# Second norm's row gather two ticks earlier, its statistics in the middle of a chunk, in a two-layer gated cross-attention kernel

## The reference

```python
x = x + jnp.tanh(g_xattn[0]) * _L0_xattn_ref(_layernorm(x, axis=-1), ctx_1024, ctx_1024, ...)
x = x + jnp.tanh(g_ffn[0]) * _L0_ffn_ref(_layernorm(x, axis=-1), ...)
x = x + jnp.tanh(g_xattn[1]) * _L1_xattn_ref(_layernorm(x, axis=-1), ctx_1024, ...)
x = x + jnp.tanh(g_ffn[1]) * _L1_ffn_ref(_layernorm(x, axis=-1), ...)
```

## Time and profile before

| | before |
|---|---|
| median of 3 runs | 1305.31 us (1303.09 to 1306.69) |
| the profiled execution | 1305.32 us |
| its span | 1303.6 us |
| PE busy | 1113.0 us (85%) |
| DVE busy | 1010.9 us (78%) |
| POOL busy | 637.0 us (49%) |
| ACT busy | 586.5 us (45%) |
| mean granted clock of PE | 0.959 of full speed |

### The profile page before, as it was taken

How to read it: one execution, slowest core, us unless ns; L and a number is a source line. 1 busy time by engine, 2 the same in 40 slices (tenths; PEclk the granted TensorE clock), 3 DMA queues, 4 the chain that set the end, 5 groups by cost and what they waited for, 6 DMA issues and landing times.

```text
span 1303.6 us, 23736 instructions
## 1 busy us (share of the span) xinstructions
PE 1113.0 (85%) x7464; PEld 960.2 (74%) x7464; DVE 1010.9 (78%) x2393; ACT 586.5 (45%) x1506; POOL 637.0 (49%) x377
## 2 busy tenths in 40 slices
PE   5145544899969998799889999999999999999998
PEld 3133333789858988688788888889888888888887
DVE  2999999989999899898537444445688888888887
ACT  2212222465636555355454645454344444444443
POOL 4889997898788987899340110101011111111200
PEclk9999985799989999799899999999999999999999
DMA  6101112889748886589666255552000000000000
GB/s 226 49 25 41 40 41 73 264 269 284 224 151 263 278 253 208 187 240 294 189 198 206 78 176 160 174 162 79 22 25 25 25 25 25 26 25 25 26 9 17
DMA packets 125035, 166.41 MB, mean 128 GB/s; under 512 B 10032, under 2 KB 67568, under 8 KB 124912
## 3 DMA queue, kind: packets, MB, share of 16 engines
q1 hardware_dynamic: 119792, 152.31, 38.1%
q0 software_dynamic: 5120, 12.59, 2.9%
HBM read 137.60 MB, written 27.26 MB: 126 GB/s over the span
## 4 chain that ended last, share of the span: by engine, by line
PE 56%; DVE 25%; issue 8%; POOL 7%; ACT 2%; DMA 1%; SPq 0%; DVEq 0%; POOLq 0%; ACTq 0%
PE ZB L1276 8%; DVE q_sb L898 6%; PE YB L1290 6%; PE YD L1328 5%; DVE s L873 4%; PE ZD L1244 4%; PE ZD L1246 4%; PE ZD L1245 4%; POOL prod L586 3%; PE YB L1328 3%; PE ZB L1244 2%; DVE own_prod L862 2%; PE ZB L1246 2%; PE ZB L1245 2%; POOL xs L596 2%
## 5 line engine op out<-in xcount | busy, mean ns | idle before, releaser
L562 POOL TENSOR_TENSOR rstd<-ve,neghalf 128x4 f32<-128x4 f32 x64 | 65.6, 1025 | 516.6 <-DVE ve L827 515.2
L683 ACT ACTIVATE hid<-ZB,w2b 128x128 f32<-128x128 f32 x768 | 215.8, 378 | 159.0 <-PE YB L1290 78.5
L574 POOL TENSOR_TENSOR prod<-q_sb,kv_sb 128x2048 f32<-128x2048 f32 x48 | 216.3, 4507 | 51.9 <-DVE q_sb L898 31.6
L586 POOL TENSOR_TENSOR prod<-s,kv_sb 128x2048 f32<-128x2048 f32 x48 | 215.2, 4505 | 10.6 <-DVE q_sb L898 10.5
L1276 PE MATMUL ZB<-bt,w1b 128*128 128x128 f32 x1536 | 213.2, 284 | 4.9 <-ACT hid L683 4.7
L1276 PEld LDWEIGHTS ZB<-bt,w1b 128*128 128x128 f32 x1536 | 197.0, 200 | 8.5 <-issue 8.0
L1290 PE MATMUL YB<-w2b,hid 128*128 128x128 f32 x1024 | 141.4, 282 | 0.0
L1290 PEld LDWEIGHTS YB<-w2b,hid 128*128 128x128 f32 x1024 | 129.1, 194 | 14.2 <-ACT hid L683 8.0
L705 ACT ACTIVATE own_prod<-ZD 128x512 f32<-128x512 f32 x102 | 61.1, 599 | 154.6 <-PE ZD L1246 152.3
L1095 DVE TENSOR_TENSOR prod<-own_prod,ZD 128x512 f32<-128x512 f32 x102 | 69.5, 682 | 75.0 <-ACT own_prod L705 51.7
L1110 DVE SCALAR_TENSOR_TENSOR own_prod<-YD,gate,own_prod 128x128 f32<-128x128 f32 x320 | 89.7, 342 | 46.5 <-PE YD L1328 44.6
(11 more groups left out here) (249 smaller groups left out, 2321.0 us busy)
## 6 DMA issues: line engine op xcount, KB each, us to landing
w2b<-in_w SPq DMA_DIRECT2D x96, 516.0 KB
w1b<-in_w SPq DMA_DIRECT2D x96, 512.0 KB
xb<-xs SPq DMA_DIRECT2D x96, 128.0 KB
ctx_t<-in_ctx SPq DMA_DIRECT2D x32, 256.0 KB
x2d<-x2s SPq DMA_DIRECT2D x48, 128.0 KB
x<-in_x SPq DMA_DIRECT2D x16, 256.0 KB
xs<-zrow SPq DMA_DIRECT2D x4, 1024.0 KB, 10.5
xrow<-in_x SPq DMA_DIRECT2D x16, 256.0 KB, 3.6
```

Source lines behind the costliest of these rows:

```text
L574: pool.tensor_tensor(out=prod[:, t % 2, :].rearrange("p (h e d) -> p h e d", h=HEADS, e=HEADS), in0=q.unsqueeze(2).broadcast_to([P, HEADS, ...
L586: pool.tensor_tensor(out=prod[:, (t + 1) % 2, :].rearrange("p (h d e) -> p h d e", h=HEADS, e=HEADS), in0=s0[:, t, :, :].unsqueeze(2).broa ...
L683: act.activation(hid[n % 2][:, j, k * RT:(k + 1) * RT], ZB[j // 2][:, at:at + RT], ACT.Relu, bias=w2b[t % 3][:, k, e, FJ * D + j:FJ * D + ...
```

## The change

The gather is issued two ticks earlier (kc = -6 and -5), POOL's small norm one tick earlier (kc = -2), and DVE's statistics move from kc = -2, even half, to kc = -4, odd half. `_ready` in the table of start ticks is raised by two.

```diff
@@ -72,7 +72,7 @@
-    _ready = max(h for h, (b, _) in PLACE.items() if b == BLOCK_OF[_c]) // 2 + 5
+    _ready = max(h for h, (b, _) in PLACE.items() if b == BLOCK_OF[_c]) // 2 + 7
     C0.append(max(_ready, C0[-1] + 8 if C0 else 8 * (NC + 1)))
@@ -95,7 +95,7 @@
 def c_parts(tick):
-    return [(c, tick - C0[c]) for c in range(NC) if -4 <= tick - C0[c] < 8]
+    return [(c, tick - C0[c]) for c in range(NC) if -6 <= tick - C0[c] < 8]
@@ -615,7 +615,7 @@
                     for c, kc in c_parts(tick):
-                        if kc == -1:
+                        if kc == -2:
                             norm(2, c)
@@ -631,9 +631,9 @@
                     for c, kc in c_parts(tick):
-                        if kc == -4:
+                        if kc == -6:
                             gather(c, (0, 1))
-                        if kc == -3:
+                        if kc == -5:
                             gather(c, (2, 3))
@@ -1187,10 +1187,6 @@
                     for c, kc in c_parts(tick):
-                        if kc == -2:
-                            for j in range(TILES):
-                                dve.wait_ge(ld_x2[j].sem, ld_x2[j].at(c))
-                            norm_stats(2, lambda j: x2[c % 2][:, j, :], c)
                         if kc == 2:
                             biased(BVV, vv_sb, "vv", c)
@@ -1202,6 +1198,10 @@
                             logits_max(d)
                     for c, kc in c_parts(tick):
+                        if kc == -4:
+                            for j in range(TILES):
+                                dve.wait_ge(ld_x2[j].sem, ld_x2[j].at(c))
+                            norm_stats(2, lambda j: x2[c % 2][:, j, :], c)
                         if kc == 1:
                             score_max(c)
```

## The result

The changed kernel takes **1326.34 us** (median of 4 runs, 1318.66 to 1329.51) where the kernel before took 1306.0 beside it (1303.09 to 1307.68): ratio 1.0144, 95% interval 1.0123 to 1.0164, that is 18.8 us (16.1 to 21.4) more. The forecast was 1314.8 with a range up to 1319.0. The sign was right, the forecast rise (9.5 us) about half of what came, and the time lies above the range. The profiled execution took 1324.97 us.

What follows compares the result with a forecast made beforehand. PE was taken to set the pace in the last stage (97% busy), any hold on it paid in full. 1305.3 - 4.0 (front) + 13.5 (last stage), chunks 1 to 5 at 0, gave 1314.8 us, range 1309.0 to 1319.0.

Steps and rivals of the forecast that it cites:

- The last stage, +13.5 us: Ten chunks: statistics delay unit 7's product and PE; nine chunks at 1.40 us plus 0.9 for the first; 10.8 to 14.5.
- none of the 1.46 us is absorbed, nine of ten alike: Last stage: nine of ten chunks have no DVE gap between L1019 and unit 7's product, so all pay.
- Rival 1: Last stage: DVE's idle 18% swallows the 1.46 us, only the front counts, faster at 1301.3 us; chance 0.08.
- rival 2: Last stage: earlier statistics remove PE's 0.56 us wait for xn in ten chunks, giving 1309.2 us; chance 0.06.
- Rival 3: Last stage: a 1.3 us wait in each chunk lowers PE's clock, 2.2 us more in ten chunks, 1336.8; chance 0.03.
- Rival 4: Front: gathers land as late relative to DVE as before, scatters standing between, no gain, 1318.8 us; chance 0.03.
- The front, chunk 0, -4.0 us: First attention to cross attention: PE reaches L1391 2.8 us earlier, plus 1.2 us for the clock; -1.5 to -5.0.
- the last of eight such DMAs starts 7 x 1.27 us after 598.67: Front, POOL's queue: last gather starts at 607.6, rows usable at 611.8, DVE waits about 1.5 us in place of 4.89.
- my 3.7: Front, chunk 0: PE's new wait for DVE's later work, 0.73 + 3.0 = 3.7 us.
- let DVE hide by half: Front: a clock drop behind PE's new wait is half hidden by PE waiting for DVE anyway; 1.2 us counted.
- Chunks 1 to 5, cost 0: While experts run: statistics ahead of x2s still leave it made in time; otherwise 1.46 us in each of four chunks.

Runs made afterwards that it cites:

- last_only: Kernel before with the whole change for chunks 6 to 15 only, chunks 0 to 5 as before: 1319.01 us, 1.0098.
- pos4: Kernel before with chunks 6 to 15 alone altered: statistics right behind the value bias, in DVE's idle gap, gathers at kc = -9 and -8: 1305.76 us, 0.9996.
- c0_only: Kernel before with the whole change for chunk 0 alone: 1304.85 us, 0.9986.
- c0_spread: Kernel before with chunk 0 alone changed, its gathers still earlier (kc = -8, -7), a POOL product between and behind the pairs: 1304.47 us, 0.9982.
- c1_kept: Kernel before with the change for chunks 0 and 2 to 5, chunk 1 and chunks 6 to 15 as before: 1304.06 us, 0.9991.
- all_but_c1: Changed kernel with chunk 1 alone as in the kernel before: 1319.15 us, 1.0097.
- c0_and_c1: Kernel before with the whole change for chunks 0 and 1 only: 1311.12 us, 1.0039.
- eight_in_a_row: Kernel before with four added gathers into an unread tile behind the real four from chunk 8 on, making runs of eight: 1346.69 us, 1.0303.
- c1_to_5: Kernel before with the whole change for chunks 1 to 5, chunk 0 as before: 1309.31 us, 1.0008.
- gather_only: Kernel before with only POOL's gathers moved in all chunks, norm and statistics where they were: 1306.71 us, 1.0006.
- c1_gather_only: Kernel before with the whole change for chunk 0 and only the gathers moved for chunk 1: 1312.01 us, 1.0045.
- front_only: Kernel before with the whole change for chunks 0 to 5, chunks 6 to 15 as before: 1313.36 us, 1.0048.
- spread: Kernel before with the change for chunks 0 to 5, but their gathers further ahead (kc = -8, -7); chunks 6 to 15 as before: 1313.83 us, 1.0059.
- no_two_port: Kernel before with the change for chunks 0 to 5, where nmean and ve are made by scalar_tensor_tensor in place of tensor_scalar: 1315.56 us, 1.0058.
- combined: Kernel before with chunk 0 as in c0_spread, chunks 1 to 5 as before, chunks 6 to 15 as in pos4: 1303.22 us, 0.9982.

## Why the prediction was right in part and wrong in size

**The last stage, +13.5 us: right.** last_only measured 12.8 us and the trace 13.0. The step "none of the 1.46 us is absorbed, nine of ten alike" held: chunks of 33.74 against the 33.7 named, 1.41 us each against 1.40. The first chunk cost 0.35 in place of 0.9, since DVE's gaps took up 0.94 us and not 0.5. The matmuls took 1.13 where I had 1.16. pos4 shows the reason by its opposite: it is the place ahead of a product that PE asks for 0.12 us later, not the ten instructions.

**Rival 1 (all hidden) and rival 2 (the xn wait given back)** are excluded by the nine new waits at L1328 and by the xn wait that stays. **Rival 3 (the clock falls in the last stage)** is excluded: nine waits of 1.2 us, and 1.00 throughout. The rule of the Trainium skill, TensorE: Matmul & The Clock Gate, section A second HAM failure mode: psum-queue depth-cycling, did not apply to idles of this size and spacing. **Rival 4 (the gathers land too late)** is excluded as well: the first statistics start at 608.03 us without a wait.

**The front, chunk 0, -4.0 us: right in sign, too large.** c0_only measured -1.8 (-3.7 to -0.1). The 4.89 us wait is gone and L1391 is not held, but L1391 is not nearly 3 us earlier: counted from the landmark at 601 us it comes 1.1 us later in the changed kernel. (Only c0_spread, whose gathers stand elsewhere, has it at 627.09, where I had 627.2; that is luck.) Three prices were missing. I had worked out that "the last of eight such DMAs starts 7 x 1.27 us after 598.67", so I had the run of eight before me, and charged it to POOL alone; ACT stood 6 us beside it, and PE waited 5.48 us in place of my 3.7. The half speed behind that wait, 0.55 from 609 to 618 us or 4.1 us of work, I had let DVE hide by half; the rank matmul then found its tile ready, so nothing was hidden. And nmean, taken at 0.17 us from the steady rows, met POOL's product, whose place I had in the earlier trace rows, and took 2.69 us. What is left as a gain is that L1391 now runs at full speed, where it stood at the head of a slow stretch before. The windows do not settle how much: the profiled execution of c0_only was its slowest, 1309.21 us.

**Chunks 1 to 5, cost 0: this is the step that failed.** It holds for chunks 2 to 5 as long as chunk 1 stays (c1_kept). For chunk 1 it is wrong by 6 to 7 us: 6.1 from all_but_c1, and (1.0039 - 0.9986) x 1306 = 6.9 from c0_and_c1 against c0_only. I had asked there only where the statistics stand on DVE (ahead of x2s, whose reader comes later) and had not followed chunk 1's four gathers through POOL's queue, where they now stand around chunk 14's scatters. My own steps had even brought these scatters forward, by making pick_slots 3.4 us early (629.72 to 626.3). The terms as measured apart: -1.8 for chunk 0, +6.9 for chunk 1, 0 for chunks 2 to 5 and +12.8 make +17.9, against 18.8 (16.1 to 21.4) measured.

**What stays open.** That eight indirect transfers in a row stop the other engines is shown, in the last stage alone and in the front; by what they do it is not. The trace of the changed kernel has no load of instructions from 598 to 612 us, and that of eight_in_a_row none from 1063 to 1070, so that isn't it. That chunk 0 and chunk 1 must both move for the loss is shown (c1_to_5 and c0_only against c0_and_c1), and that it takes chunk 0's statistics and chunk 1's gathers (gather_only against c1_gather_only). That this is because chunk 14's scatters then close up to the gathers ahead of them, and because PE no longer has its wait for pick_slots to hide a standstill in, is what the traces suggest (POOL's pause between the first two gathers and the scatters is 1.1 us in front_only, 2.7 in gather_only and in c1_to_5), but no run separates the two.

## What to carry to other kernels

An instruction that moves takes its own queue with it: follow every transfer that the step issues, and look at what will stand next to it there, not only at who waits for its data. Short work on an engine that is 18% idle is free or costs its full length depending on whether the next tile it delays has a reader at the door, so look for the gap, then for the reader. And where a trace shows engines idle for "remote" on a kernel of one core, look at what the other engines were issuing in that moment.

## What the runs showed of the hardware that I had not expected

- A run of eight indirect transfers from POOL, 1.27 us apart, stops ACT, DVE and PE from about the fifth on: 4.95 us a run in the last stage with the DMA engines 0.11 busy, lower clock included, and 2.3 to 6.1 us of ACT in the front. With a pause of 2.8 us after four, 0.7 us are left. Four in a row stop ACT too, for 1.8 us in three places of the kernel before.
- A DVE instruction on four elements a partition takes as long as POOL's running product still has: 1.6 to 3.4 us for nmean and once 4.5 for ve, in place of 0.17, with `tensor_scalar` as with `scalar_tensor_tensor`. The reductions and products of DVE on larger tiles beside it ran at their usual time. By the Trainium skill, SBUF — State Buffer, section Who interferes with whom, the shared port pair is held for a whole instruction and not divided; the ends agree, within 0.1 us in the changed kernel, gather_only, spread and no_two_port.
- After a wait of 3.3 us PE ran at half speed for some 9 us, after one of 2.1 us it did not. The wait's length alone does not tell, as two traces at other places show: behind 2.80 us in combined eight matmuls took 2.05 us, and behind only 1.22 us in c0_spread they took 1.67:

```profile
613.99 2.05 PE L1276 MATMUL ZB<-bt,w1b 128*128 128x128 f32 x8 [2.80 <-ACT hid L683]
...
609.98 1.67 PE L1276 MATMUL ZB<-bt,w1b 128*128 128x128 f32 x8 [1.22 <-ACT hid L683]
```
